# The image a sample ahead, half of each group norm's second part on ScalarE, diagonals on ScalarE

## The reference

```python
x = x + L0(gn(x))   # 3x3 depthwise conv, Mamba-2 block (ssd), 3x3 depthwise conv, MLP
x = x + L1(gn(x))   # in_proj, 3x3 depthwise conv, selective scan in 4 directions, norm, out_proj
x = x + L2(gn(x))   # 3x3 depthwise conv and bias
x = x + L3(gn(x))   # 3x3 depthwise conv and bias

def _gn(v, G=32, eps=1e-5):
    g = v.reshape(B_, H_, W_, G, C_ // G)
    m = jnp.mean(g, axis=(1, 2, 4), keepdims=True)
    s = jnp.var(g, axis=(1, 2, 4), keepdims=True)
    return ((g - m) / jnp.sqrt(s + eps)).reshape(v.shape)
```

## Time and profile before

| | us |
|---|---|
| median of 3 runs | 27994.83 |
| lowest and highest | 27981.98, 28007.52 |
| the profiled execution's own time | 27990.44 |
| its span | 27988.9 |
| PE, DVE, ACT, POOL busy | 24871.7, 23791.4, 21025.9, 21307.0 |

### The profile page before, as it was taken

How to read it: one execution, slowest core, us unless ns; L and a number is a source line. 1 busy time by engine, 2 the same in 40 slices (tenths; PEclk the granted TensorE clock), 3 DMA queues, 4 the chain that set the end, 5 groups by cost and what they waited for, 6 DMA issues and landing times. The chain is left out here.

```text
span 27988.9 us, 298606 instructions
## 1 busy us (share of the span) xinstructions
PE 24871.7 (89%) x83552; PEld 12176.8 (44%) x83552; DVE 23791.4 (85%) x23376; ACT 21025.9 (75%) x39400; POOL 21307.0 (76%) x9542
## 2 busy tenths in 40 slices
PE   8899888998889988899888998889988899888998
PEld 3444334443344433444334443344433444334443
DVE  6799867998679986799867998679986799867998
ACT  4799647996479964799647996479964799647996
POOL 3799737997379973799737997379973799737997
PEclk8999989999899998999989999899998999989999
DMA  0121101211011110111101221011110111101111
GB/s 8 48 61 61 44 8 48 61 61 44 8 48 61 61 44 8 48 61 61 44 8 48 61 61 44 8 48 61 61 44 8 48 61 61 44 8 48 61 61 44
DMA packets 796830, 1243.08 MB, mean 44 GB/s; under 512 B 220800, under 2 KB 238080, under 8 KB 792064
## 3 DMA queue, kind: packets, MB, share of 16 engines
q1 hardware_dynamic: 795136, 1223.32, 14.6%
HBM read 1155.89 MB, written 67.11 MB: 44 GB/s over the span
## 5 line engine op out<-in xcount | busy, mean ns | idle before, releaser
L1593 PE MATMUL ps<-arena,ident 128*128 128x512 f32 x24576 | 11621.7, 597 | 80.4 <-POOL arena L1978 80.4
L1408 DVE TENSOR_TENSOR_SCAN arena<-arena,ps 128x512 f32<-128x512 f32 x6912 | 8322.0, 1253 | 2.0 <-issue 2.0
L1408 DVE TENSOR_TENSOR_SCAN arena<-ps,arena 128x512 f32<-128x512 f32 x5376 | 6493.6, 1256 | 97.7 <-ACT ps L1790 97.7
L1968 POOL TENSOR_TENSOR arena<-arena 128x1536 f32<-128x1536 f32 x1792 | 6181.4, 3457 | 36.2 <-DVE arena L1408 35.1
L1593 PEld LDWEIGHTS ps<-arena,ident 128*128 128x128 f32 x24576 | 4350.9, 190 | 4267.9 <-issue 3788.1
L1978 POOL TENSOR_TENSOR arena<-arena 128x1536 f32<-128x1536 f32 x1728 | 5977.8, 3463 | 205.0 <-ACT arena L1810 203.5
L1801 ACT ACTIVATE scaled<-arena,cols 128x384 f32<-128x384 f32 x9216 | 5245.7, 607 | 963.9 <-PE ps L1561 931.8
L1790 ACT ACTIVATE arena<-arena 128x512 f32<-128x512 f32 x6912 | 4779.8, 715 | 14.4 <-PE ps L1593 13.3
L1561 PE MATMUL ps<-ident,scaled 128*128 128x128 f32 x27648 | 4009.3, 277 | 764.4 <-DVE arena L1408 631.0
L1561 PEld LDWEIGHTS ps<-ident,scaled 128*128 128x128 f32 x27648 | 3169.4, 141 | 3258.3 <-DVE arena L1408 1736.1
L1790 ACT ACTIVATE ps<-arena 128x512 f32<-128x512 f32 x5376 | 3570.7, 679 | 334.9 <-DVE arena L1408 300.1
(11 more groups left out here) (187 smaller groups left out, 32508.5 us busy)
## 6 DMA issues: line engine op xcount, KB each, us to landing
arena<-rows SPq DMA_DIRECT2D x3520, 256.0 KB, 3.3
spare<-rows SPq DMA_DIRECT2D x576, 256.0 KB, 3.3
arena<-x SPq DMA_DIRECT2D x16, 1536.0 KB, 13.1
x<-arena SPq DMA_DIRECT2D x16, 1536.0 KB, 10.7
arena<-x SPq DMA_DIRECT2D x64, 384.0 KB, 8.4
out<-arena SPq DMA_DIRECT2D x64, 384.0 KB, 3.0
rows<-xd SPq DMA_DIRECT2D x256, 64.0 KB, 2.8
arena<-L_conv_fc_w SPq DMA_DIRECT2D x16, 576.0 KB, 5.3
```

The lines of the kernel that those rows point to most:

```text
L1408: nc.vector.tensor_tensor_scan(flip(states(b, n, t)), flip(decays), flip(adds), carry[:, k, N2 * n + t:N2 * n + t + 1], ALU.mult, ALU.add) ...
L1593: nc.tensor.matmul(m.ps[:, t, :], m.ident[:, :], states(b, n, t), start=False, stop=(n == SUMS[t][-1])).then_inc(at[Y_MM[t]], 1)
L1968: nc.gpsimd.tensor_tensor(three(dbu[:, no % DB, :]), du[:, b % 2, :, :], each, ALU.mult).then_inc(at["db_ready"], 1)
```

## The change

Three edits go together.

- The image of the next sample is loaded during the last convolution of this one, into slots 6 and 7 (`xin`), ahead of the eight stores on SyncE's queue. The first image is loaded in a stage of its own before the loop, by one transfer. Norm 0 reads `xin`, and ScalarE copies it to `s01` (`keep`), where the later residual is expected. The input has one more image at its end (a copy of the first) for the last sample's load.
- In every norm, VectorE writes the first half and a quarter of the second one; ScalarE writes the other three quarters of it, as `rstd * x + shift`, with `shift = -mean * rstd` from a new small VectorE operation.
- The diagonals of the four norms are built by ScalarE (`Taps.scalar`), behind its part of the norm, and not by GpSimd. The diagonals that are built in the ssd stage stay with GpSimd.

```diff
-def group_norm(m, src, dst, taps, load=None, loads=(), have_stats=False):
+def group_norm(m, src, dst, taps, loads=(), have_stats=False, keep=None):
...
+    shift = m.take(NH, parts=P)
+    cut = L // 4
...
         def _(sp):
-            for h in range(NH):
-                if load is not None:
-                    sp.dma_start(src[:, h, :], load[:, h, :]).then_inc(loaded[h], 16)
             taps.sync(sp, taps_loaded)
             bring(m, sp, brought, loads)
-
-        @block.gpsimd
-        def _(pool):
-            taps.gpsimd(pool, taps_loaded, centre)
...
-                if load is not None:
-                    dve.wait_ge(loaded[h], 16)
...
-            for h in range(NH):
-                nc.vector.tensor_scalar(dst[:, h, :], src[:, h, :], m.gn_mean[:, h:h + 1], m.gn_rstd[:, h:h + 1],
+            nc.vector.scalar_tensor_tensor(shift, m.gn_mean[:, :], -1.0, m.gn_rstd[:, :], ALU.mult, ALU.mult).then_inc(shift_done, 1)
+            for h, end in ((0, L), (1, cut)):
+                nc.vector.tensor_scalar(dst[:, h, 0:end], src[:, h, 0:end], m.gn_mean[:, h:h + 1], m.gn_rstd[:, h:h + 1],
                                         ALU.subtract, ALU.mult)
 
         @block.scalar
         def _(act):
+            if keep is not None:
+                for h in range(NH):
+                    nc.scalar.copy(keep[:, h, :], src[:, h, :])
             act.wait_ge(rstd_in, 1)
             nc.scalar.activation(m.gn_rstd[:, :], m.gn_rstd[:, :], ACT.Sqrt).then_inc(rstd_out, 1)
+            act.wait_ge(shift_done, 1)
+            nc.scalar.activation(dst[:, 1, cut:], src[:, 1, cut:], ACT.Identity, scale=m.gn_rstd[:, 1:2], bias=shift[:, 1:2])
+            taps.scalar(act, taps_loaded, centre)
...
+    def scalar(self, act, loaded, centre):
+
+        nc, w = self.m.nc, self.w
+        act.wait_ge(loaded, 32)
+        if self.own:
+            nc.scalar.activation(w[:, :, 4:5], w[:, :, 4:5], ACT.Identity, bias=1.0).then_inc(centre, 1)
+            act.wait_ge(centre, 1)
+        for t in range(self.n):
+            for i, tap in enumerate(PE_TAPS):
+                nc.scalar.activation(self.diag[:, t * len(PE_TAPS) + i, :], self.m.ident[0:self.parts, 0:self.parts], ACT.Copy,
+                                     scale=w[:, t, tap:tap + 1])
...
         def _(sp):
-            bring(m, sp, brought, loads)
             if out is not None:
+                for to, of in loads:
+                    sp.dma_start(to, of).then_inc(brought, 16)
                 for i, (t, r) in enumerate(steps):
                     sp.wait_ge(side_added, i + 1)
                     sp.dma_start(rows(out, t, r), rows(dst, t, r)).then_inc(stored, 16)
+                sp.wait_ge(brought, 16 * len(loads))
                 sp.wait_ge(stored, 16 * len(steps))
+            else:
+                bring(m, sp, brought, loads)
...
+        xin = m.slots(6, NH, P)
+        with Stage(nc, "first_in") as (first_in,), nc.Block() as block:
+            @block.sync
+            def _(sp):
+                sp.dma_start(xin, x[0].rearrange("(t p) l -> p t l", p=P)).then_inc(first_in, 16)
+                sp.wait_ge(first_in, 16)
         with nc.Fori(0, samples) as b:
-            xb = x[bass.ds(b, 1)].rearrange("a (t p) l -> p (a t) l", p=P)
+            x_next = x[bass.ds(b + 1, 1)].rearrange("a (t p) l -> p (a t) l", p=P)
...
-            group_norm(m, s01, s23, taps, load=xb)
+            group_norm(m, xin, s23, taps, keep=s01)
...
-            conv3x3(m, s23, s01, taps, residual=s45, out=ob, **ONE)
+            conv3x3(m, s23, s01, taps, residual=s45, out=ob, loads=[(xin[:, h, :], x_next[:, h, :]) for h in range(NH)], **ONE)
...
     if name == "x":
         v = v.transpose(0, 3, 1, 2).reshape(v.shape[0], C, L)
+        v = np.concatenate([v, v[:1]])
```

More of the change, by code:

```diff
@@ L172, in group_norm @@
     dev = m.take(NH, parts=P)
-    names = ("loaded_0", "loaded_1", "stats_done", "mean_mm", "var_in", "var_mm", "chain", "rstd_in", "rstd_out",
-             "brought") + Taps.NAMES
-    with Stage(nc, *names) as (*loaded, stats_done, mean_mm, var_in, var_mm, chain, rstd_in, rstd_out, brought,
+    shift = m.take(NH, parts=P)
+    cut = L // 4
+    names = ("stats_done", "mean_mm", "var_in", "var_mm", "chain", "rstd_in", "rstd_out", "shift_done", "brought") + Taps.NAMES
+    with Stage(nc, *names) as (stats_done, mean_mm, var_in, var_mm, chain, rstd_in, rstd_out, shift_done, brought,
                                taps_loaded, centre), nc.Block() as block:
```

## The result

The changed kernel takes 27872.34 us (median of 5 runs, 27863.78 to 27879.87) against 27994.83 us before (5 runs, 27981.98 to 28007.52): 0.9956 of it, 95% interval 0.9942 to 0.9971, so 122 us or 0.44% faster. The forecast was 27880. The profiled executions are 27874.2 us of span after and 27988.9 before, 114.7 us apart.

A forecast was written before the change was run, and what follows sets the result against it. Each group-norm stage is bounded by its last engine between barriers. Norm 0 -73.9, first sample +6.8, norms 1 to 3 -48.2, together -115.3 us; with 4.4 from profile to median, 27880 us, range 27840 to 27930.

The forecast's parts named there:

- The last engine of each norm: Group-norm stages: norm 0 waits for the image load, then VectorE; VectorE ends norm 3, GpSimd's diagonals end norms 1 and 2.
- rival C: Norms 1 and 2 gain nothing, as another wait (taps' or w_in's transfer) ended them: 27932 us; chance 0.04.
- The chain behind the reciprocal: From the reciprocal's end to the next stage: shift, ScalarE's 3072 columns in 2.81 us, diagonals 2.25 or 3.6, barrier 0.29.
- The four sums: Reciprocal's end to next stage: norm 0 5.83 us, norm 3 5.58, norm 2 5.58, norm 1 6.93.
- Rival A: ScalarE's work in the norms at upper bounds, 3.32 us and no overlap of diagonals: +45, 27925 us; chance 0.08.
- The rule against the split: Norms: moving work off a faster VectorE pays only if it is saturated; forecast still had the split gain 1.5 us.
- The load: Norm 0 no longer waits for the image: 19.06 us instead of 29.62, 10.56 less in 7 of 8 samples.
- The draining: Norm 0's table loads: some 1.38 us more per switch, with slow copies +10 us over 7 samples; forecast kept 0.
- rival D: Last convolution: engines stand still while the image streams in, 134 us, giving 28014, or 28147 if doubled; chance 0.03.
- B: Norm 0 keeps its length because something else holds the start of the sample: 27954 us; chance 0.05.
- The first sample: Its load in a stage of its own: norm 0 starts at 21.5 us, convolution at 40.6 instead of 33.80, +6.8.

The follow-up runs named there:

- the diagonals alone: Against the kernel before, only the norms' diagonals moved from GpSimd to ScalarE, behind the square root; VectorE writes both halves: 27908.31 us, 0.9972.
- the kernel with the smaller part: Changed kernel with GpSimd's diagonals in norms 0 and 3; in norms 1 and 2 ScalarE's diagonals first, its part 896 and 1792 columns: 27816.1 us, 0.9937.
- the split alone: Against the kernel before, only ScalarE's three quarters of each norm's second half; load and GpSimd's diagonals as before: 27917.51 us, 0.9973.
- the kernel with twice the copies: Changed kernel, but ScalarE copies the image twice in norm 0, the second time into two free slots: 27901.08 us, 0.9967.
- the double load: Changed kernel, but the last convolution loads the image twice, the second time into two free slots: 27871.45 us, 0.9958.
- GpSimd's diagonals in norms 0 and 3: Changed kernel, but in norms 0 and 3 GpSimd builds the diagonals beside the statistics, as before the change: 27842.57 us, 0.9948.
- the load alone: Against the kernel before, only the image load moved into the last convolution; norms whole on VectorE, diagonals on GpSimd: 27911.78 us, 0.9973.
- the load and diagonals without the split: Changed kernel, but VectorE writes both halves and ScalarE builds the diagonals behind the square root: 27832.52 us, 0.9944.
- the ssd block's diagonals: On the kernel with the smaller part, ScalarE also builds the eight diagonals of the ssd block's opening stage: 27766.48 us, 0.992.

## Why the prediction was right

**The last engine of each norm.** Right in all four. That GpSimd ended norms 1 and 2 (rival C) was argued from its last diagonal's end; the diagonals alone gave 71.6 us there.

**The chain behind the reciprocal.** ScalarE's 3072 columns took 2.95 us, not 2.81. The slope of 0.86 ns was about right: 896, 1792 and 3072 columns of this form take 1.12, 1.87 and 2.95 us in the kernel with the smaller part, 0.84 ns a column, and 4096 columns of a plain copy took 3.60 (3.69 forecast). The fixed part was mis-sized. By that slope it is 0.37 us here and 0.16 for the copy; this form takes its scale and its shift from an operand each. The Trainium skill (ScalarE: Activation LUTs, What ACT_TABLE_LOAD costs) adds some 0.09 us for each such operand and comes to 2.93; the trace agrees. What made up for it is that the next operation starts 0.10 us before this one ends (3519.76 against 3519.86), which the sum left out. The centre tap took 0.22 with its wait instead of 0.25, the eight diagonals 2.21 to 2.23 instead of 2.25 and the twelve 3.60 instead of 3.6. The four sums came out within 0.05 us, by two small errors against each other and so in part by luck. Rival A, the upper bounds, is out.

**The rule against the split.** By the rule of the Trainium skill (Perfetto Trace Analysis, Optimizing Scalar/DVE Operations) the part given to ScalarE is slower than on VectorE, and it is: 2.95 us against the 1.6 that VectorE saved. The split alone still made norms 0 and 3 1.53 us shorter, as both halves run side by side. The Trainium skill is also milder there than I had it: with VectorE saturated, moving work "may make sense". What counted was the combination: with the diagonals behind it, the split cost some 29 us in the norms that the kernel without it keeps. I had priced that (0.5 to 0.8 us a norm) but had not drawn the conclusion that in norms 1 and 2, too, it turned 5.05 into 6.9 and 5.6.

**The load.** Norm 0 and the turn of the loop gave 75.4 us of 73.9, and that closeness, too, is made of two errors: the stage itself gave 72.4, as its statistics start up to 0.6 us after its first operation, which norm 3's don't, and 2.9 came from the last convolution, 0.4 us shorter in each sample, which the forecast put at nothing. The copies and both table loads stayed covered; the slack was 3.1 to 3.7 us instead of 2.7. The draining of which the Trainium skill tells behind a table load (ScalarE: Activation LUTs, What ACT_TABLE_LOAD costs) doesn't appear where it would have: the kernel with twice the copies has the square root 0.01 us after the load. The convolution beside the transfer lost nothing, nor with twice the transfer, so rival D is out, and B with it. In the last convolution of the first sample both halves had landed at 3454.87, before the second store's issue at 3464.66, as forecast.

**The first sample.** +6.2 for +6.8: the load landed and the stage was left at 20.9, not 21.5.

**What the sum left out.** The 7.8 us between the profiled difference (114.7) and that of the medians (122.5) is within the spread of the runs. It was luck that the ssd stage kept its 464 us in seven of eight samples (467.4 in the last): the kernel with the split alone shows that an edit elsewhere can move it by 8 us a sample. That last sample put 3.4 us into the 2.7 between the norms. My range of 27840 to 27930 did not price this at all.

## What to carry to other kernels

Between barriers, look for the engine that ends last and ask what it could have done before the last common wait. Work that has no need of the norm's result (the diagonals) belongs ahead of it or beside it, not behind the piece that was just moved to the same engine, and what is moved should be no larger than lets both engines end together. Here order and size were worth 29 us together, a quarter of the whole gain (by the estimate above mostly the size), and dropping the split, the most elaborate of the three edits, beat keeping all. A change that moves a stage's start may move an untouched stage behind it that hangs on TensorE by more than itself: compare stage by stage, and the granted clock with it, before an experiment is believed.

## What the runs showed of the hardware that was not expected

- **A stage of fixed work has several lengths.** The ssd stage takes 456 to 473 us with the same instructions, and by and large the length goes with TensorE's granted clock (0.87 to 0.82 of full speed on average over the stage, the engine being at either 1.2 or 2.4 GHz at any moment). It is steady, at 464 us, in the kernel before, with the diagonals alone, in the kernels with GpSimd's diagonals in norms 0 and 3, with the smaller part, with the double load and with the double copies, and, but for one sample, in the changed kernel; it is mixed with the load alone, the split alone, the load and diagonals without the split, and the ssd block's diagonals. In this stage TensorE pauses again and again for the other engines, and the clock falls and comes back many times: in the second sample 14 stretches at the lower level in the kernel before, 12 with the split alone. What decides which length a sample gets was not found; no experiment here held the start of that stage and changed nothing else. The traces give one pointer, an observation and not a cause: in the ten kernels whose opening stage is the old one, the convolution ahead of it took 51.5 to 52.5 us in 65 of 80 samples, and in 64 of these the ssd stage took 463.7 to 464.6 us. In the other 15 the convolution took 50.8 to 51.4 us or 52.9, and there the ssd stage took anything from 457 to 473.
- **Time given back behind a norm.** The projection behind norm 1 and the last convolution open on TensorE products at the lower clock, and the moment at which it rises doesn't follow the stage's start. For the projection behind norm 1 it rises 3.9 us after the stage's start with the diagonals alone, 4.9 in the kernel before, 5.4 in the changed kernel and 6.5 with the split alone, and from its start to the next convolution's first long ScalarE operation the stage takes 44.4, 44.9, 45.2 and 45.7 us: half a us more for each us that the clock comes later. The last convolution shows the same: 56.6, 57.0, 57.4 and 57.6 us with the rise at 4.2 (changed kernel), 5.0 (before), 5.9 (split alone) and 6.2 us (GpSimd's diagonals in norms 0 and 3). With the split alone norm 1 ended 1.6 us earlier and the stretch to norm 2's reciprocal was 1.3 to 1.7 us longer in every sample; the projection is 0.8 of that, and the rest was not followed. In the changed kernel 0.25 to 0.6 of 3.9 came back there in seven samples and nothing in the other; with the diagonals alone that stretch got 0.8 to 1.0 us shorter in seven of eight.
